# QKV, gate, up and down products of a decoder layer: one plain fp32 matmul in place of three products of high and low parts

## The reference

```python
h = layernorm(x)
Q = h @ Wq.T + bq;  K = h @ Wk.T + bk;  V = h @ Wv.T + bv      # 256 -> 256 each
scores = (g * (Q @ W_cross) . K + (1 - g) * Q . (M @ K)) * scale   # per head, causal
x = x + softmax(scores) @ V @ Wo.T + bo
x = x + cross_attention(layernorm(x), ctx, mask)               # not touched
h = layernorm(x)
gate = h @ (w_gate / 127).T;  up = h @ (w_up / 127).T          # 256 -> 768 each
x = x + (silu(gate) * up) @ (w_down / 127).T                   # 768 -> 256
```

## Time and profile before

| what | value |
|---|---|
| median of 3 runs | 1248.72 us (1245.33 to 1255.58) |
| span of the profiled execution, first to last instruction | 1246.4 us, at a mean granted clock of 0.935 |
| PE busy | 1081.7 us, 87% of the span |
| DVE, ACT, POOL busy | 792.2, 557.3, 216.0 us |

### The profile page before, as it was taken

The page is one execution under the profiler, slowest core; times in us unless marked ns, Lnnn a source line. Parts: engine busy times, 40 slices in busy tenths (PEclk is TensorE's granted clock), DMA queues, the critical chain, the costliest instruction groups (busy, mean ns, idle before and its releaser), DMA issues. The chain is left out here.

```text
span 1246.4 us, 23540 instructions
## 1 busy us (share of the span) xinstructions
PE 1081.7 (87%) x7116; PEld 640.1 (51%) x7164; DVE 792.2 (64%) x1705; ACT 557.3 (45%) x1022; POOL 216.0 (17%) x175
## 2 busy tenths in 40 slices
PE   1888969998999899999998665769999689999997
PEld 1677424443444344444443443434444278888886
DVE  4799837776777777777781775745555255555452
ACT  2456126665666666666666111216666321111110
POOL 4155510000000000000001233310000133333321
PEclk9899769998999989999999777859999889999999
DMA  6389892443344434444022578885666422222200
GB/s 196 104 289 309 252 149 70 85 91 71 75 86 87 87 69 86 86 87 90 18 74 87 170 218 234 245 235 148 173 177 163 148 68 68 68 67 67 67 18 34
DMA packets 132838, 153.30 MB, mean 123 GB/s; under 512 B 29003, under 2 KB 104319, under 8 KB 132735
## 3 DMA queue, kind: packets, MB, share of 16 engines
q1 hardware_dynamic: 126207, 145.74, 45.5%
q10 hardware_dynamic: 6528, 6.29, 1.5%
HBM read 87.69 MB, written 64.95 MB: 122 GB/s over the span
## 5 line engine op out<-in xcount | busy, mean ns | idle before, releaser
L687 DVE TENSOR_REDUCE self_pm<-bank 128x1 f32<-128x512 f32 (+3 forms) x608 | 365.4, 656 | 100.0 <-PE bank L772 68.7
L738 ACT ACTIVATE self_prob<-bank 128x512 f32<-128x512 f32 (+1 forms) x608 | 325.6, 577 | 184.1 <-PE bank L794 110.1
L786 PE MATMUL bank<-self_stq,self_stk 98*128 98x512 bf16 (+3 forms) x768 | 225.7, 334 | 24.9 <-DMA self_stq<-self_mrow 11.8
L763 PE MATMUL bank<-self_stk,self_stq 96*128 96x512 bf16 (+3 forms) x768 | 228.7, 342 | 8.1 <-DVE self_mrow L684 5.4
L806 PE MATMUL bank<-self_prob,self_va 128*32 128x512 f32 (+3 forms) x1536 | 163.7, 507 | 4.3
L763 PEld LDWEIGHTS bank<-self_stk,self_stq 96*128 96x128 bf16 x768 | 71.2, 100 | 162.4 <-DVE self_pm L687 111.8
L961 POOL TENSOR_TENSOR rin<-rin,bo_b 128x1024 f32<-128x1024 f32 x8 | 26.1, 3259 | 538.1 <-DMA min_<-mask_BxSxS_bk 538.1
L1768 ACT ACTIVATE e_sg<-bank 128x512 f32<-128x512 f32 x48 | 28.7, 599 | 191.9 <-PE bank L184 191.9
L786 PEld LDWEIGHTS bank<-self_stq,self_stk 98*128 98x128 bf16 x768 | 70.1, 99 | 83.8 <-issue 32.0
L738 ACT ACTIVATE cross_prob<-bank 96x512 f32<-96x512 f32 x128 | 74.8, 593 | 63.2 <-PE bank L791 63.0
L687 DVE TENSOR_REDUCE cross_pm<-bank 128x4 f32<-128x384 f32 x128 | 70.0, 557 | 35.0 <-PE bank L768 33.2
(11 more groups left out here) (189 smaller groups left out, 1423.9 us busy)
## 6 DMA issues: line engine op xcount, KB each, us to landing
qk<-a_parts SPq DMA_DIRECT2D x32, 384.0 KB, 4.8
self_stq<-qk SPq DMA_DIRECT2D x192, 64.0 KB, 2.9
self_stk<-qk SPq DMA_DIRECT2D x96, 128.0 KB, 5.2
cross_stq<-xqs SPq DMA_DIRECT2D x32, 384.0 KB, 4.7
vs<-a_vst SPq DMA_DIRECT2D x8, 1024.0 KB, 5.5
self_va<-vs SPq DMA_DIRECT2D x16, 512.0 KB, 7.0
od<-self_u SPq DMA_DIRECT2D x16, 512.0 KB, 2.7
oin<-od SPq DMA_DIRECT2D x32, 256.0 KB
```

The costliest lines, as they stand in the source:

```text
L687: nc.vector.tensor_reduce(pm[:, k, h0:h0 + hb, r], src[:, 0:hb * w].rearrange("p (h w) -> p h w", h=hb), AX, ALU.max).then_inc(s_mxe, 1)
L738: nc.scalar.activation(ops.prob[:, u % NPS, 0:hb * n], bank[ST_BANKS[u % 3]][0:KP, 0:hb * n], ACT.Exp).then_inc(s_ex, 1)
L763: mm = nc.tensor.matmul(dst[:, h * w:(h + 1) * w], stq[i][0:R, half, h0 + h, r * P:(r + 1) * P], stk[i][0:R, h0 + h, k0:k0 + w], start=(h ...
L786: mm = nc.tensor.matmul(dst[0:KP, h * n:(h + 1) * n], stk[i][0:RM, h0 + h, kt * KP:(kt + 1) * KP], stq[i][0:RM, half, h0 + h, q0:q0 + n], ...
```

## The change

`cut_products` becomes `products`, which issues one matmul for each slice of the contraction on plain fp32 operands. The tiles lose their high/low axis and the float32r type, ACT writes one fp32 tile and signals `s_xt` itself, and all instructions that make low parts go: `low` in the preparation, `turned_low` in QKV and feed-forward, the cast at line 1715 and `hidden_low` on POOL. DVE writes the product of silu and up straight into `ht`, and `down` waits for that (`s_h`). No other instruction changes its place in any engine's order.

```diff
-        def cut_products(dst, terms):
-            n = 0
-            for a, b in terms:
-                for i, j in ((0, 0), (0, 1), (1, 0)):
-                    mm = nc.tensor.matmul(dst, a[:, i], b[:, j], start=(n == 0), stop=(n == 3 * len(terms) - 1))
-                    n += 1
+        def products(dst, terms):
+            for n, (a, b) in enumerate(terms):
+                mm = nc.tensor.matmul(dst, a, b, start=(n == 0), stop=(n == len(terms) - 1))
             return mm
...
-        wq_t = sb("wq_t", [P, 2, KT, D], F32R)
+        wq_t = sb("wq_t", [P, KT, D])
...
-                        nc.vector.tensor_tensor(lo, bank[n % NB][:, 0:w], hi.bitcast(F32), ALU.subtract).then_inc(s_el, 1)
...
-                        if n - NB in cut:
-                            t_.wait_ge(s_el, cut.index(n - NB) + 1)
...
                 t_.wait_ge(s_e, N_CTX)
-                t_.wait_ge(s_el, len(cut))
...
-            xnt = sb("a_xnt", [P, 2, 2, KT, CH], F32R)
+            xnt = sb("a_xnt", [P, 2, KT, CH])
...
-                def turned_low(b, u):
-                    c = 2 * b + u
-                    for k in range(KT):
-                        v.wait_ge(s_xh, 2 * c + k + 1)
-                        nc.vector.tensor_tensor(xnt[:, u, 1, k], bank[k][:], xnt[:, u, 0, k].bitcast(F32),
-                                                ALU.subtract).then_inc(s_xt, 1)
...
-                        nc.scalar.activation(xnt[:, u, 0, k], bank[k][:], ACT.Identity).then_inc(s_xh, 1)
+                        nc.scalar.activation(xnt[:, u, k], bank[k][:], ACT.Identity).then_inc(s_xt, 1)
...
-                        m = cut_products(bank[QKB[n]][:],
-                                         [(w_[:, :, k, (n % 2) * P:(n % 2 + 1) * P], xnt[:, u, :, k]) for k in range(KT)])
+                        m = products(bank[QKB[n]][:],
+                                     [(w_[:, k, (n % 2) * P:(n % 2 + 1) * P], xnt[:, u, k]) for k in range(KT)])
...
-                def hidden_low(b, u, h):
-                    c = 2 * b + u
-                    g.wait_ge(s_hh, HT * c + h + 1)
-                    nc.gpsimd.tensor_tensor(ht[:, u, 1, h], hf[:, h % 2], ht[:, u, 0, h].bitcast(F32),
-                                            ALU.subtract).then_inc(s_hl, 1)
...
-                    v.wait_ge(s_hl, HT * c + h + 1)
-                    nc.vector.tensor_tensor(hf[:, h % 2], bank[5 + 2 * (h % 2)][:], sg[:, h % 2], ALU.mult).then_inc(s_h, 1)
-                    v.wait_ge(s_h, 2 + HT * c + h + 1)
-                    nc.vector.tensor_copy(ht[:, u, 0, h], hf[:, h % 2]).then_inc(s_hh, 1)
...
+                    nc.vector.tensor_tensor(ht[:, u, h], bank[5 + 2 * (h % 2)][:], sg[:, h % 2], ALU.mult).then_inc(s_h, 1)
...
-                    t.wait_ge(s_hl, 2 + HT * (c + 1))
+                    t.wait_ge(s_h, 2 + HT * (c + 1))
...
-                            mm = cut_products(bank[OB[w]][:, i * D:(i + 1) * D],
-                                              [(ht[:, u, :, h, tok], wd_t[:, :, h]) for h in range(HT)])
+                            mm = products(bank[OB[w]][:, i * D:(i + 1) * D],
+                                          [(ht[:, u, h, tok], wd_t[:, h]) for h in range(HT)])
```

More of the change, by code:

```diff
@@ L29 @@
 F32 = mybir.dt.float32
-F32R = mybir.dt.float32r
 BF16 = mybir.dt.bfloat16
@@ L122, in program @@
         negid = sb("negid", [SK, HG, SK], BF16)
-        wq_t = sb("wq_t", [P, 2, KT, D], F32R)
-        wk_t = sb("wk_t", [P, 2, KT, D], F32R)
-        wv_t = sb("wv_t", [P, 2, KT, D], F32R)
+        wq_t = sb("wq_t", [P, KT, D])
+        wk_t = sb("wk_t", [P, KT, D])
+        wv_t = sb("wv_t", [P, KT, D])
         wo_t = sb("wo_t", [P, KT, D])
@@ L132, in program @@
         bo_b = sb("bo_b", [P, D])
-        wg_t = sb("wg_t", [P, 2, KT, HID], F32R)
-        wu_t = sb("wu_t", [P, 2, KT, HID], F32R)
-        wd_t = sb("wd_t", [P, 2, HT, D], F32R)
+        wg_t = sb("wg_t", [P, KT, HID])
+        wu_t = sb("wu_t", [P, KT, HID])
+        wd_t = sb("wd_t", [P, HT, D])
         mhalf = sb("mhalf", [P, J])
@@ L271, in program @@
             s_e = sem("w_e")
-            s_el = sem("w_el")
             s_kh = sem("w_kh")
@@ L286, in turned @@
                         jobs.append(([src[:, o + i, k * P:(k + 1) * P] for i in range(n)],
[L287 to L294, removed]
+                                     dst[:, k, o * P:(o + n) * P]))
+            turned(n_k, wk_t, KT, KT)
+            turned(n_v, wv_t, KT, KT)
+            turned(n_o, wo_t, KT, KT)
             n_small = len(jobs)
-            turned(fg, both(wg_t), KT, HT)
-            turned(fu, both(wu_t), KT, HT)
-            turned(fd, both(wd_t), HT, KT)
+            turned(fg, wg_t, KT, HT)
+            turned(fu, wu_t, KT, HT)
+            turned(fd, wd_t, HT, KT)
             NJ = len(jobs)
-            cut = [n for n in range(NJ + KT) if n >= NJ or len(jobs[n][1]) == 2]
             N_FOLD = NJ + KT
@@ L377, in _ @@
             def _(v):
[L378 to L387, removed]
-                        nc.vector.tensor_tensor(lo, bank[n % NB][:, 0:w], hi.bitcast(F32), ALU.subtract).then_inc(s_el, 1)
-                    made[0] = upto
                 v.wait_ge(s_in, 16 * N_IN)
@@ L426, in _ @@
                 normalise1(v, 0, 0)
-                low(len(cut))
                 v.wait_ge(s_g, 14)
@@ L456, in _ @@
                             nc.scalar.activation(f[:], i[:], ACT.Identity, scale=WSCALE).then_inc(s_f, 1)
-                    empty(n, dst[0], bank[n % NB][:, 0:len(blocks) * P])
+                    empty(n, dst, bank[n % NB][:, 0:len(blocks) * P])
                 for k in range(KT):
-                    empty(NJ + k, wq_t[:, 0, k, :], bank[(NJ + k) % NB][:, 0:D])
+                    empty(NJ + k, wq_t[:, k, :], bank[(NJ + k) % NB][:, 0:D])
                 empty(N_FOLD, qkb[:, 0, :], bank[N_FOLD % NB][:, 0:KT])
@@ L1127, in chunk @@
                     split(b, u, 1)
-                    if more:
-                        turned_low(nb, nu)
                     if again(b):
@@ L1226, in values @@
                         tok = slice((2 * w + i) * P, (2 * w + i + 1) * P)
-                        m = cut_products(bank[VB[w]][:, i * D:(i + 1) * D],
-                                         [(xnt[:, u, :, k, tok], wv_t[:, :, k]) for k in range(KT)])
+                        m = products(bank[VB[w]][:, i * D:(i + 1) * D],
+                                     [(xnt[:, u, k, tok], wv_t[:, k]) for k in range(KT)])
                     m.then_inc(s_vm, 1)
@@ L1560, in program @@
         s_tr = sem("e_tr")
-        s_xh = sem("e_xh")
         s_xt = sem("e_xt")
@@ L1565, in program @@
         s_h = sem("e_h")
-        s_hh = sem("e_hh")
-        s_hl = sem("e_hl")
         s_y = sem("e_y")
@@ L1574, in credits3 @@
             for s_, n in ((ffn_in.s_on, 2), (s_op, 4), (s_xn, 8), (s_tr, 4), (s_xt, 2), (s_gu, 12), (s_sg, 2),
-                          (s_h, 2), (s_hl, 2), (s_y, 4), (s_yo, 4)):
+                          (s_h, 2), (s_y, 4), (s_yo, 4)):
                 sp.sem_inc(s_, n)
@@ L1648, in program @@
             yo = sb("e_yo", [P, 2, J, D])
-            xnt = sb("e_xnt", [P, 2, 2, KT, CH], F32R)
+            xnt = sb("e_xnt", [P, 2, KT, CH])
             sg = sb("e_sg", [P, 2, CH])
-            hf = sb("e_hf", [P, 2, CH])
-            ht = sb("e_ht", [P, 2, 2, HT, CH], F32R)
+            ht = sb("e_ht", [P, 2, HT, CH])
             block = st.enter_context(nc.Block())
@@ L1689, in chunk @@
                         power3(g, b + u, 1 - u)
-                    hidden_low(b, u, 2)
-                    hidden_low(b, u, 3)
-                    hidden_low(b, u, 4)
                     if again(b):
                         ffn_in.quotients(g, b + 1, u)
[L1695 to L1701, removed]
                 sweep(g, chunk)
@@ L1761, in turned @@
                         a.wait_ge(s_tr, 4 + 2 * c + k + 1)
-                        nc.scalar.activation(xnt[:, u, 0, k], bank[TB[k]][:], ACT.Identity).then_inc(s_xh, 1)
+                        nc.scalar.activation(xnt[:, u, k], bank[TB[k]][:], ACT.Identity).then_inc(s_xt, 1)
                 def silu(b, u, h):
@@ L1803, in gate_up @@
                     for w_, o in ((wg_t, 4), (wu_t, 5)):
-                        mm = cut_products(bank[o + 2 * (h % 2)][:],
-                                          [(w_[:, :, k, h * P:(h + 1) * P], xnt[:, u, :, k]) for k in range(KT)])
+                        mm = products(bank[o + 2 * (h % 2)][:],
+                                      [(w_[:, k, h * P:(h + 1) * P], xnt[:, u, k]) for k in range(KT)])
                     mm.then_inc(s_gu, 1)
```

3 lines of the change are left out of this document (removed).

## The result

The changed kernel takes 1295.35 us in the median of 4 runs (1292.95 to 1295.74), the kernel before 1250.61 (1245.33 to 1255.58, 4 runs): a ratio of 1.037, 95% interval 1.033 to 1.041. The forecast was 1294. The profiled execution took 1295.45 us with a span of 1293.7, 47.3 us more than the span before.

What follows compares the result with a forecast made beforehand. PE was taken to bound the feed-forward stage, with PE, DVE and DMA all close to full in QKV. Feed-forward +41.4 and QKV +3.5 gave 45 us, a forecast of 1294 us, range 1286 to 1306.

Steps and rivals of the forecast that it cites:

- The prices: PE: a plain product takes 0.860 us at 512 columns, 0.431 at 256, adding 0.158 and 0.071 us.
- Feed-forward, +41.4: Feed-forward stage: 5.5 us more per chunk, 44.0 over eight chunks, less 0.8 and 1.8 at the ends.
- The two ends: Feed-forward start and end: PE no longer waits for low part, cast and subtraction, saving 0.8 and 1.8 us.
- QKV, +3.5 of 2.0 to 5.1: QKV stage: PE's longer chunks delay the values by 5.1 us, of which 2.0 to 5.1 reach self attention; middle taken.
- a queue of stores: QKV to self attention: the barrier waits for stores to land, so slower chunks may not delay first scores fully.
- the lower bound: QKV: if the store queue is the bound, only the shift at chunk 4 is passed on, 2.0 us.
- the middle of the two bounds: QKV: 3.5 us taken between 2.0 and 5.1, since slower chunks also leave the queue less behind.
- The slack of 0.1 us: QKV chunk: DVE's normalised chunk ready 3.3 us after the values, just under the 3.44 us of queries on PE.
- rival (a): QKV: DVE stays late and the queue hides nothing, so all cost shows; sum 54 us, 1303 us; 8%.
- (b): PE: instructions count, not passes, so plain products take two thirds; faster, about 1168 us; 2%.
- (c): PE: removed weight loads were the cost, giving back 42 of 44 feed-forward us; 1248 us, no change; 2%.
- (d): Feed-forward: denser fp32 work gets a lower clock, its 270 us of PE growing by up to as much again; 3%.

Runs made afterwards that it cites:

- the bf16 matmuls in the runs: Kernel before with high and low parts in bf16 instead of float32r: in feed-forward 1228.58 us, ratio 0.985; in QKV too 1231.32 us, ratio 0.991.
- the run with that part alone: Kernel before with only gate, up and down products made plain fp32, QKV as before: 1284.89 us, ratio 1.030.
- The kernels with fewer products: Changed kernel's low-part work removed, but two or one float32r matmuls per product on the rounded copy: 1173.34 us with two, 1127.05 us with one.
- QKV alone: Kernel before with only QKV products made plain fp32, gate, up and down as before: 1255.81 us, ratio 1.007.
- the run with two products: Against the kernel without low parts, which has three float32r matmuls per product, two per product, counting the high product twice: 1173.34 us.

## Why the prediction was right

**The prices.** 0.430 and 0.216 us for a plain instruction came from the output product and the cross queries of the kernel before, eight or sixteen in a row; in streams of 24 and 48 they are 0.429 and 0.216. The price of the operation after was in the trace before, because the kernel already had it at another place. The rule of N/2.4 + 2.5 ns of the Trainium skill (page "TensorE: Matmul & The Clock Gate", section "Back-to-back issue gap"), by which the sum would have been 64 us, agrees with the bf16 matmuls in the runs (0.216 and 0.109) but not with the float32r ones (0.234 and 0.120) that the change removes; that difference is where it overstates.

**Feed-forward, +41.4.** Measured 41.4 in the changed kernel and 41.3 in the run with that part alone. The two ends gave back 0.7 and 1.8 us (0.8 and 1.8 forecast). Prices, path and ends were all as forecast; this part is no luck.

**QKV, +3.5 of 2.0 to 5.1.** The chunk of 11.17 us came as 11.2, and the end of the stage moved by 5.2 (5.1 forecast). That is closer than its terms: the first queries start 1.7 us earlier (1.15 forecast), and the chunks add 6.9 us (6.2 forecast), since the first one grew by 2.3 and not 1.8. The first scores moved by 2.7, inside the bounds and nearer the lower one. Executions with the same QKV products differ there by 1.5 us (165.7 to 167.2), so one profile cannot tell 2.7 from 3.5.

The reason given was a queue of stores that holds the handover and is less far behind when chunks are slower. The timeline of SP in the changed kernel, beside the earlier trace rows, bears it out:

```profile
133.26 0.63 SPq L1058 DMA_DIRECT2D vs<-a_vst  x1
135.09 6.66 SPq L1053 DMA_DIRECT2D qk<-a_parts  x4
141.79 0.89 SPq L1058 DMA_DIRECT2D vs<-a_vst  x1
151.42 5.50 SPq L938 DMA_DIRECT2D self_stq<-qk  x12
```

Here SP pauses for 1.2 us before the last chunk's stores (133.89 to 135.09), while in the kernel before it issues without a pause from 119 us to the last store. So it is less behind. The last store lands 9.5 us after its issue, at 151.3, for 10.4 us and 148.6 in the kernel before, and in both the next loads follow within 0.2 us. So the landing, the loads and the first scores all move by 2.6 or 2.7 us, while the values move by 5.2. The kernels with fewer products show the same queue holding the first scores while the values end up to 11.6 us earlier. The step of the forecast that was only guessed is its size: the lower bound took the shift at chunk 4 as the whole, and the middle of the two bounds was a choice and not a sum.

The slack of 0.1 us that the prediction gave DVE was in truth larger, because normalising sped up by 0.9 us, which I had not foreseen, and that left rival (a) less room. The prediction put PE's wait of 1.19 us down to a DVE that is nearly full; about 0.9 us of it were POOL's subtraction.

**What was not in the sum.** From the first scores to the end of self attention the shift goes from 2.7 to 5.7 us, in instructions that are the same. It changes in three short stretches: down to 1.7 by 191 us of the kernel before, up to 3.0 near 305 us, and up to 5.7 near 440. The windows over the last of them, cut at the same instructions (length, busy PE, PEld, DVE, ACT, POOL, granted clock, DMA share, GB/s), show how. First before, then after:

```profile
434.69:445.93 11.24, 10.50 (x64) 4.96 (x66) 4.41 (x8) 5.78 (x11) 0.00 (x0) 0.70 0.32 84
```

```profile
437.65:451.64 13.99, 11.34 (x65) 5.17 (x66) 4.41 (x8) 5.89 (x11) 0.00 (x0) 0.63 0.22 58
```

DVE has the same work to the hundredth, ACT within 0.1 us, and the granted clock is 0.63 for 0.70: within the stretch PE is at the lower of its two levels (1.2 GHz) for about 10 us, where it was for about 7. The stretch is 2.75 us longer. In the 119 us before it the shift does not move by 0.1 us. Self attention, first scores to the start of the last product, lasted 510.9 to 521.3 us in the ten profiled executions here, with the same instructions in each, at a granted clock of 0.98 in the shortest and 0.96 in the longest. The 3 us lie within that spread. That they owe nothing to the change is not shown: both kernels with plain QKV products took 519 us, and QKV alone cost 8 us in the medians (interval 5 to 12) with 3.5 us at the first scores. The total fell onto 45 us partly by luck: 41.4 + 2.7 + 3.2 = 47.3 in the spans, while the medians differ by 44.7. The prediction had left this to the spread of the runs.

**Rivals.** (a), all of QKV's cost shows: no. (b), instructions count: no, 0.429. (c), the load: no, by the trace and by the run with two products. (d), the clock: 0.99 in the stage as before.

## What to carry to other kernels

Price a new operation by the distance between its instructions where the kernel already has it, and price the old one the same way; a rule that holds for one type can miss another by a tenth. Fewer instructions and less work on two other engines bought nothing where PE was alone on the path, and a plain fp32 product takes as long as four bf16 passes against three float32r ones. What the other engines' work was worth showed only where PE waited for it: at the two ends of a stage, and in the stage where DVE was full. And where a barrier waits for stores to land, look at the last landing: it, and not the last product, may be what the next stage follows.

## What the runs showed of the hardware that was not expected

- A DVE instruction that takes 0.40 us alone took 1.29 and 0.91 us where it began beside a POOL subtraction on full tiles, and ended 0.15 us after that in both kernels. POOL work that looked free cost 5 us before the first maxima (129.5 for 134.5 once POOL's operands were cut to 16 columns).
- A float32r matmul with its load is 8% slower than a bf16 one of 512 columns (0.234 to 0.216) and 10% slower at 256 (0.120 to 0.109). A plain fp32 instruction is not: 0.429 is two of 0.216.
- The length of self attention varied by 10 us between executions with identical instructions (510.9 to 521.3), with the granted clock in short stretches (0.70 and 0.63 in the one shown).
- The last store of QKV landed 9.5 to 10.4 us after its issue in the three kernels read here, and the first scores followed that landing: with the values 11.6 us earlier they came 1.3 us earlier.
